# Two state-space (Mamba) stages: decay factors written to PSUM and scanned in halves of 512, and the B rows spread by DMA

## The reference, cut to what matters

```python
def mamba(x, in_w, conv_w, conv_b, xproj_w, dt_w, dt_b, Alog, Dp, out_w):
    ...
    dbl = jnp.einsum('bld,ed->ble', xs, xproj_w)
    dt, Bc, Cc = jnp.split(dbl, [dt_rank, dt_rank + D_STATE], axis=-1)
    dt = jax.nn.softplus(jnp.einsum('blr,dr->bld', dt, dt_w) + dt_b)
    A = -jnp.exp(Alog)
    dA = jnp.exp(dt[..., None] * A)
    dBx = dt[..., None] * Bc[:, :, None, :] * xs[..., None]

    def step(h, inp):
        dA_t, dBx_t, C_t = inp
        h = dA_t * h + dBx_t
        y = jnp.einsum('bds,bs->bd', h, C_t)
        return (h, y)
    ...
    y = ys.transpose(1, 0, 2) + Dp * xs
    y = y * silu(z)
    return jnp.einsum('bld,od->blo', y, out_w)
```

## Time and profile before

| what | value |
|---|---|
| median of 3 runs | 12151.99 us (12149.31 to 12155.65) |
| profiled execution, span | 12171.0 us; no other time is given for this execution |
| its mean granted TensorE clock | 0.790 |
| the two Mamba stages | about 4775 to 6325 and 6325 to 7885 us of the span |
| busy in these 3110 us | DVE 2778.7, PE 2153.1, POOL 1756.2, ACT 1443.8 us |

### The profile page before, as it was taken

How to read it: one execution, slowest core, us unless ns; L and a number is a source line. 1 busy time by engine, 2 the same in 40 slices (tenths; PEclk the granted TensorE clock), 3 DMA queues, 4 the chain that set the end, 5 groups by cost and what they waited for, 6 DMA issues and landing times. The chain is left out here.

```text
span 12171.0 us, 160668 instructions
## 1 busy us (share of the span) xinstructions
PE 8871.1 (73%) x60596; PEld 5530.5 (45%) x60686; DVE 8283.4 (68%) x10689; ACT 4218.5 (35%) x5843; POOL 2710.7 (22%) x807
## 2 busy tenths in 40 slices
PE   6667888576767566676666776678767788886789
PEld 4445655344445422222223333256544566664566
DVE  6655234577778745999978988845676666666654
ACT  3333123211110044444444444443333333333333
POOL 0000000043446502555555565500000000000000
PEclk7777666566677777788888888899878999996689
DMA  0000000000000000000000000000000000000000
GB/s 17 0 10 7 3 1 0 13 0 0 0 0 0 7 1 4 0 0 0 0 4 0 0 0 0 0 9 8 4 0 2 15 2 2 2 2 10 6 9 14
DMA packets 44978, 46.01 MB, mean 4 GB/s; under 512 B 11435, under 2 KB 33558, under 8 KB 43958
## 3 DMA queue, kind: packets, MB, share of 16 engines
q1 hardware_dynamic: 44726, 42.24, 1.3%
HBM read 35.93 MB, written 6.29 MB: 3 GB/s over the span
## 5 line engine op out<-in xcount | busy, mean ns | idle before, releaser
L2066 DVE TENSOR_TENSOR_SCAN m_hs<-m_dA,m_dBx 128x1024 f32<-128x1024 f32 x516 | 1599.2, 3099 | 180.9 <-POOL m_dBx L1764 161.2
L1764 POOL TENSOR_TENSOR m_dBx<-m_dtx,m_Bs 128x1024 f32<-128x1024 f32 x516 | 1402.5, 2724 | 1197.3 <-ACT m_Bs L1947 596.4
L1873 PE MATMUL m_ps_y<-m_yc,ident 128*128 128x512 f32 x2064 | 1274.2, 751 | 41.2 <-DVE m_yc L2072 38.1
L2408 PE MATMUL x_ps_p<-Y,ident 128*128 128x256 f32 (+1 forms) x1920 | 713.5, 546 | 384.2 <-DVE Y L2325 214.8
L1947 ACT ACTIVATE m_Bs<-m_ps_B 128x512 f32<-128x512 f32 x516 | 306.7, 594 | 1546.5 <-PE m_ps_B L1851 1313.3
L1854 PE MATMUL m_ps_C<-m_parts,m_sel 128*128 128x512 bf16 x488 | 224.7, 460 | 779.1 <-DVE m_yc L2072 772.8
L2408 PEld LDWEIGHTS x_ps_p<-Y,ident 128*128 128x128 f32 x1920 | 428.2, 244 | 662.0 <-issue 236.0
L1873 PEld LDWEIGHTS m_ps_y<-m_yc,ident 128*128 128x128 f32 x2064 | 499.1, 242 | 435.5 <-issue 384.3
L2072 DVE TENSOR_TENSOR m_yc<-m_hs,m_ps_C 128x1024 f32<-128x1024 f32 x516 | 630.0, 1221 | 89.5 <-issue 83.0
L1950 ACT ACTIVATE m_dA<-m_dt,m_A 128x504 f32<-128x504 f32 x1032 | 676.3, 705 | 0.8
L547 POOL MEMSET c_vbd<- 128x1152 f32 x2 | 2.1, 1063 | 2937.0 <-POOLq L56 2937.0
(11 more groups left out here) (696 smaller groups left out, 20283.0 us busy)
## 6 DMA issues: line engine op xcount, KB each, us to landing
c_kvb<-in_ctxT SPq DMA_DIRECT2D x50, 256.0 KB, 2.7
out_dram<-X SPq DMA_DIRECT2D x1, 4096.0 KB
c_table<-in_table SPq DMA_DIRECT2D x2, 512.0 KB
focus_rows<-X SPq DMA_DIRECT2D x2, 512.0 KB, 9.5
x_xb<-in_ctx SPq DMA_DIRECT2D x1, 1024.0 KB, 15.1
x_xa<-focus_rows SPq DMA_DIRECT2D x1, 1024.0 KB, 7.3
focus_out<-x_hat_a SPq DMA_DIRECT2D x1, 1024.0 KB, 3.8
Y<-focus_out SPq DMA_DIRECT2D x2, 512.0 KB
```

What stands on the lines that cost most here:

```text
L1764: return nc.gpsimd.tensor_tensor(to, one, other, ALU.mult)
L1873: last = nc.tensor.matmul(ps_y[:, m, :], C.ident[:], yc[:, s % 2, m, :], start=s == 0, stop=s == NS - 1)
L2066: nc.vector.tensor_tensor_scan(flat(h), flat(dA[:, s % R, :, :]), flat(dBx[:, s % 2, :, :]), 0.0, ALU.mult, ALU.add).then_inc(scanned, 1)
L2408: last = nc.tensor.matmul(sum_bank(c)[:, 0:width], C.ident[:], parts[:, :, e], start=e == 0, stop=e == n - 1)
```

## The change

**Decay and scan.** ScalarE writes each half of `dA` into one of three PSUM banks (`ps_dA`, half h = 2s + m goes to bank h mod 3) instead of the SBUF ring. The scan is two instructions of 512 elements with one operand in PSUM and one in SBUF. `scanned` and `decay` now count halves; ScalarE may write half h once half h - 3 has been scanned (h - 2 for the first two halves of a group).

**C.** The three banks come from `ps_B` (two) and the second bank of `ps_C`. `spread_C` for state s + 1 is now issued once `yc` of state s has been written.

**B.** `spread_B` on TensorE and the copy on ScalarE are gone. ScalarE copies the 16 f32 rows of B once per group to `low` (with the rows it copied before), SyncE stores them to a DRAM tensor `B_rows` (32 KB), waits for that, and loads them back two rows at a time, each spread over 128 partitions (`Bs`, 512 KB per DMA, 8 DMAs per group, 4 slots). The DMA of a slot waits until GpSimd has used the slot's last two rows. `sel` keeps only its C half.

```diff
+        SLOTS, CHUNK = 4, 2
+        FREE_HALVES, FREE_STATES = 3, SLOTS * CHUNK
...
-        dA, Bs = sb("dA", [P, R, NHF, GT]), sb("Bs", [P, R, GT])
+        Bs = sb("Bs", [P, SLOTS, CHUNK, GT])
...
-        ps_B, ps_C, ps_y = ps("ps_B", [P, 2, GT]), ps("ps_C", [P, 2, GT]), ps("ps_y", [P, NHF, GT])
+        ps_dA, ps_C, ps_y = ps("ps_dA", [P, 3, GT]), ps("ps_C", [P, GT]), ps("ps_y", [P, NHF, GT])
...
+            def store_B(j, par):
+                sp.wait_ge(B_low, j + 1)
+                sp.dma_start(B_rows[par], low[0:NS, :]).then_inc(B_stored, 16)
+                sp.wait_ge(B_stored, j * 16 + 16)
+                sp.sem_inc(begun, 1)
+
+            def spread_B(j, par, c):
+
+                sp.wait_ge(dBx_ready, j * NS + CHUNK * c + CHUNK)
+                rows_ = B_rows[par, CHUNK * c:CHUNK * c + CHUNK, :]
+                sp.dma_start(Bs[:, c % SLOTS, :, :], bc(rows_.unsqueeze(0), [P, CHUNK, GT])).then_inc(B_loaded[c % SLOTS], 16)
...
-            def state(n, s, par):
-
-                pool.wait_ge(B_copied, n + 3)
-                pool.wait_ge(scanned, n - 1 + R)
+            def state(j, s, par):
+
+                slot = s // CHUNK % SLOTS
+                if s % CHUNK == 0:
+                    pool.wait_ge(B_loaded[slot], j * 32 + (s // FREE_STATES * 16 + 16))
+                pool.wait_ge(scanned, j * (2 * NS) + (2 * s - 2 + FREE_HALVES))
...
-                        spread_B(n + 2, to, its)
+                        to = (s + 1) % NS
+                        its = par if to == s + 1 else 1 - par
                         front(i + 1, s, 1 - par, True)
                         if s == 9:
                             skip(par)
-                        pe.wait_ge(yc_ready, n + 1)
+                        pe.wait_ge(yc_ready, i * NS + s + 1)
                         spread_C(to, its)
-                        add_state(n, s)
+                        add_state(s)
...
-            def state(n, s, par):
-                act.wait_ge(B_done, n + 1)
-                act.wait_ge(dBx_ready, n + 1)
-                nc.scalar.activation(Bs[:, s % R, :], ps_B[:, s % 2, :], ACT.Copy).then_inc(B_copied, 1)
-                act.wait_ge(scanned, n + 1)
+            def state(j, s, par):
+
                 for m in range(NHF):
-                    last = nc.scalar.activation(seqs(dA[:, s % R, m, :]), seqs(dt[:, par, m, :]), ACT.Exp, scale=A[:, m, s:s + 1])
-                last.then_inc(decay, 1)
+                    h = 2 * s + m
+                    back = 3 if h >= 2 else 2
+                    act.wait_ge(scanned, j * (2 * NS) + (h - back + 1 + FREE_HALVES))
+                    nc.scalar.activation(seqs(ps_dA[:, h % 3, :]), seqs(dt[:, par, m, :]), ACT.Exp,
+                                         scale=A[:, m, s:s + 1]).then_inc(decay, 1)
...
-                    nc.scalar.activation(low[32:64, :], ps_j[32:64, :], ACT.Copy)
+                    if in_loop:
+                        act.wait_ge(B_stored, j * 16)
+                    nc.scalar.activation(low[0:64, :], ps_j[0:64, :], ACT.Copy).then_inc(B_low, 1)
...
-            nc.vector.tensor_copy(sel[:], bc(pick_row[:].unsqueeze(2), [P, 2 * NS, P]))
+            nc.vector.tensor_copy(sel[:], bc(pick_row[:, NS:].unsqueeze(2), [P, NS, P]))
...
-                dve.wait_ge(decay, n + 1)
-                dve.wait_ge(dBx_ready, n + 1 + R)
-                nc.vector.tensor_tensor_scan(flat(h), flat(dA[:, s % R, :, :]), flat(dBx[:, s % 2, :, :]), 0.0, ALU.mult,
-                                             ALU.add).then_inc(scanned, 1)
+                dve.wait_ge(dBx_ready, j * NS + (s + 1 + FREE_STATES))
+                for m in range(NHF):
+                    dve.wait_ge(decay, j * (2 * NS) + (2 * s + m + 1))
+                    nc.vector.tensor_tensor_scan(h[:, m, :], ps_dA[:, (2 * s + m) % 3, :], dBx[:, s % 2, m, :], 0.0, ALU.mult,
+                                                 ALU.add).then_inc(scanned, 1)
                 dve.drain()
                 if wait_free:
-                    dve.wait_ge(y_added, n - 1)
-                dve.wait_ge(C_done, n + 1)
-                nc.vector.tensor_tensor(yc[:, s % 2, :, :], h, bc(ps_C[:, s % 2, :].unsqueeze(1), both),
-                                        ALU.mult).then_inc(yc_ready, 1)
+                    dve.wait_ge(y_added, j * NS + (s - 1))
+                dve.wait_ge(C_done, j * NS + (s + 1))
+                nc.vector.tensor_tensor(yc[:, s % 2, :, :], h, bc(ps_C[:].unsqueeze(1), both), ALU.mult).then_inc(yc_ready, 1)
```

More of the change, by code:

```diff
@@ L1707, in mamba @@
         pick_row = sb("pick_row", [P, 2 * NS])
-        sel = sb("sel", [P, 2 * NS, P], BF16)
+        sel = sb("sel", [P, NS, P], BF16)
         flip = sb("flip", [P, P])
@@ L1747, in _ @@
             sp.dma_start(dt_w[rank_rows, :], W["dt_w"]).then_inc(loaded, 16)
-        n_prepared = 3
+            def store_B(j, par):
[7 more added lines that the diff above has]
+                sp.dma_start(Bs[:, c % SLOTS, :, :], bc(rows_.unsqueeze(0), [P, CHUNK, GT])).then_inc(B_loaded[c % SLOTS], 16)
+            with sp.Fori(0, C.NG // 2) as pair:
+                for par in range(2):
+                    store_B(pair * 2 + par, par)
+                    for c in range(NS // CHUNK):
+                        spread_B(pair * 2 + par, par, c)
+            store_B(C.NG, 0)
+            spread_B(C.NG, 0, 0)
+        n_prepared = 2
         @block.gpsimd
@@ L1793, in _ @@
             for s in range(AHEAD):
-                state(s, s, 0)
+                state(0, s, 0)
             with pool.Fori(0, C.NG // 2) as pair:
@@ L1846, in step_sizes @@
                 last.then_inc(dt_done, 1)
-            def spread_B(n, s, par):
-                pe.wait_ge(B_copied, n + 1)
-                nc.tensor.matmul(ps_B[:, s % 2, :], sel[:, s, :], parts[:, par, :], start=True, stop=True).then_inc(B_done, 1)
             def spread_C(s, par):
-                nc.tensor.matmul(ps_C[:, s % 2, :], sel[:, NS + s, :], parts[:, par, :], start=True,
-                                 stop=True).then_inc(C_done, 1)
+                nc.tensor.matmul(ps_C[:], sel[:, s, :], parts[:, par, :], start=True, stop=True).then_inc(C_done, 1)
             def skip(par):
@@ L1897, in _ @@
                 front(0, s, 0, False)
+            spread_C(0, 0)
             for s in range(AHEAD):
[L1899 to L1902, removed]
-                add_state(s, s)
-                spread_C(s + 2, 0)
+                pe.wait_ge(yc_ready, s + 1)
+                spread_C(s + 1, 0)
+                add_state(s)
             with pe.Fori(0, C.NG // 2) as pair:
@@ L2081, in _ @@
             for s in range(AHEAD):
-                state(s, s, False)
+                state(0, s, False)
             with dve.Fori(0, C.NG // 2) as pair:
@@ L2086, in _ @@
                     for s in range(AHEAD, NS):
-                        state(i * NS + s, s)
+                        state(i, s)
                         front(i + 1, s, 1 - par)
```

50 lines of the change are left out of this document (22 added, 28 removed).

## The result

The changed kernel took 11669.4 us in the median of four runs (11661.92 to 11683.17), the kernel before 12150.65 us beside it (12144.5 to 12155.65). The ratio is 0.9603 [0.9591, 0.9616]: 481 us less, 4.0%. The forecast was 11,730. The profiled execution has a span of 11664.5 us against 12171.0, at a granted clock of 0.800 against 0.790.

A forecast was written before the change was run, and what follows sets the result against it. VectorE, busy 89% of the two stages, was taken as the bound. From 12171.0 us: scan -392, GpSimd wait -49, preparation -49, new waits +64, sum -426, so 11745; time forecast 11,730, range 11,590 to 12,020.

The forecast's parts named there:

- The scan: VectorE's 516 scans: undisturbed half scans from PSUM, a pair 2.34 us instead of 3.10, saving 392 us (310 to 428).
- Rival 2: VectorE's scan is shut out all the same, the lock going by instruction: 83 us more, 12,235 us; chance 0.05.
- 67 us more of a dearer fixed part: Skill's rule for PSUM sources on VectorE: 1032 half scans some 65 ns dearer each, 67 us; the prediction rejected it.
- Wait for GpSimd: VectorE's waits around states 11 to 13: 1.3 and 2.2 us a group, 112 us against 161.2, 49 saved.
- Preparation: VectorE's preparation meets GpSimd's products less: e saves 30 us, `Y` 19, together 49 (0 to 100).
- as they are: VectorE's preparation instructions other than e and the first stage's `Y`: no saving counted.
- New waits: VectorE's waits for TensorE and ScalarE after stalls and clock falls: 2 us a group, 64 us added (0 to 130).
- B by DMA: Spread rows of B by DMA: transfers hidden by a factor of two, counted as zero.
- rival 3: The DMAs for B bind: at 15.1 us per spread a group takes 121 us, 12,920 us in all; chance 0.05.
- likeliest case: The forecast itself, chance 0.70, with its own range from 11,610 to 11,880 us.

The follow-up runs named there:

- matmul kernel with one state of lead: Changed kernel's half scans from PSUM, but B by matmul through one bank and ScalarE copy, its row made one state ahead: 12383.69 us, ratio 1.0195 to the kernel before.
- small product: Kernel before with GpSimd's product dBx cut to 32 of 512 columns per half, the recurrence's other input left zero: 11514.54 us, ratio 0.9464.

## Why the prediction was right, and where it was not

**The scan.** The forecast had a pair at 2.34 us and 392 us saved; the pair took 2.33 and the saving was 396. The reading behind it, that the shutting out goes by SBUF operands and not by the instruction, is shown by the ring put back into SBUF: 420 us lost with nothing else changed. Rival 2 is refuted. The 67 us more of a dearer fixed part are not there: a half scan takes 1187 ns at the least from either place. The Trainium skill gives that dearer part for a PSUM source ("VectorE: DVE Perf Modes", section on the TRN2 errata); these runs differ from it.

**Wait for GpSimd.** Right in place and in kind, both steps short: 1.70 and 2.33 us for 1.3 and 2.2. Over 32 groups that is 129 of the measured 139 us; so 22 us saved, not 49.

**Preparation.** The mechanism was right for e (1951 to 1225 ns in the mean, -24 us for -30: the forecast had taken the median of 2.18 us for the mean) and for `Y` (-21 us for -19). What I left "as they are" gained as much again: the addition of dt, the maximum, xn and a cast, 49 us together. The whole was -93 for -49, just inside its bound of 100.

**New waits.** This term was mis-sized: +64 forecast, -4 measured. I had the clock fall after each stall, from a place where VectorE stalled 3.5 us; the stalls inside a group are shorter now, TensorE was granted 0.86 in place of 0.82, and its waits never built up. ScalarE idles 1377 us on the ring of three and is still always in time. The matmul kernel with one state of lead shows that the worry was about the right thing: there VectorE idled 804 us before scans (724 put down to GpSimd, which waited for ScalarE, and 76 to ScalarE itself) and 70 before `yc` for TensorE's row of C.

**B by DMA.** "I count zero" was the step that failed. The transfers are hidden, as forecast (3.6 us landing, where one is due every 10 us, an eighth of a group; with half the slots GpSimd still waited for none), so rival 3 is out. But the copy's end also set when GpSimd's products began, and so which of VectorE's instructions they met. Taken alone it brought 135 us, on top of the PSUM scan 167. I had worked out its effect on e and on `Y`, and put it down to preparation, but I saw it as a small thing beside the scan, and with an SBUF scan it also lies in the scan itself (48 us), in the maximum (22) and in the idle time before scans (24).

**Loop turn.** Not in the sum at all: +33 us. The order of instructions showed a second wait and a second scan in each state; I did not count what that makes of a loop's body.

The forecast was 61 us high of 481, since the two terms that were too pessimistic (new waits by 68, preparation by 44) outweigh the two that were too kind (GpSimd by 27, the loop by 33). It was right for its main term; that the sum came this close is in part luck, as the errors of the small terms add up to 172 us and mostly cancel. The upper end of the likeliest case was also added up wrong: with its terms (scan -310, GpSimd -49, new waits +128) it is 11,920 us and not 11,880. The measured time lies inside either.

**What stays open.** Some 7 us of the stages. Why the granted clock rose. Of the loop's price, whether it goes by the number of instructions alone: the runs have bodies of at most 320 and of at least 330, and nothing between.

## What to carry to other kernels

When a line's single durations are spread from one value to nearly twice that beside a GpSimd at work, and those of a line with a PSUM operand are not, ask of each long VectorE instruction with two SBUF operands whether one can live in PSUM; here that place alone was worth 420 us. Where it can't, order counts: start GpSimd's work at a known point of VectorE's (a scan's end), put single two-operand instructions right at that point, ahead of it, and leave groups of small ones till it has passed; a wait taken away without looking at what it kept apart comes back as busy time. Count the instructions of a loop's body per engine, waits included, before you split one in two.

## What the runs showed of the hardware

- Which of VectorE's instructions GpSimd shuts out goes by operands: a half scan took 1187 to 1226 ns with one operand in PSUM, 1187 to 3345 with both in SBUF, in kernels alike but for that. I had not expected the maximum, with one SBUF source, to be held up as well: 0.69 to 1.75 us in the mean once GpSimd's step came one state later. It runs 1024 elements in 0.69 us, nearly twice as fast as `yc` does. The Trainium skill's "SBUF — State Buffer", section on the two separate sides, gives both kinds as takers of the shared port: two SBUF inputs, or a fast mode that uses two ports. The runs agree that both are held up; that the maximum runs in such a mode is read from its speed alone.
- A group of four small instructions loses its turn between them: xn took 0.56 us each in the mean where they come after `yc`, 0.83 where they come ahead of it, 0.34 where they met little of GpSimd (small product).
- A loop body of 330 to 352 instructions on VectorE costs some 3.3 us a turn, with packets on the instruction queue each time; one of 265 some 0.7, and with 320 and 298 the unnamed idle time before scans was 3.5 us in all, with no packet between 5000 and 6000 us.
- Of a VectorE and a GpSimd instruction that may start within 0.1 us of each other the first one runs and the other is shut out: the same addition took 1.23 us when it started 0.03 us ahead of the product and 3.40 when it started 0.04 us behind it.
- A DMA that writes the same 4 KB of DRAM to all 128 partitions, 512 KB in all, landed in 3.6 us in the median of 258, where other 512 KB transfers took 9.5, at 15% of the DMA engines' time.
